# Where the second low part of Q stands in VectorE's list, before or after the two copies of the row maxima

## The chip, the cores and the metric

The kernel runs on one core of a Trainium2 chip. The metric is the device time of one execution in microseconds (us), as the median of several runs. The core's engines each work through a list of instructions of their own, in order, and meet only at semaphores: TensorE (PE in the profile), VectorE (DVE), ScalarE (ACT), GpSimd (POOL), and SyncE (SP), which here only issues DMAs.

## The reference

The input is 16 images of 64 x 64 positions with 256 channels. For each image the layer computes

```
h1 = n1_w * arcsinh(h) + n1_b
q, k, v = split(h1 @ qkv_w + qkv_b), q scaled by hd ** -0.5     # 8 heads of 32
attn = softmax over the 3 x 3 neighbours (clipped at the edge) of q . k
h  = h + (attn @ v) @ proj_w + proj_b
h2 = n2_w * arcsinh(h) + n2_b
out = h + gelu(h2 @ mlp_w1 + mlp_b1) @ mlp_w2 + mlp_b2          # exact gelu
```

Everything is float32. The kernel gets that precision out of float16 matmuls: each value is split into a high and a low float16 part, and a product is taken as high x high, high x low and low x high.

## The kernel before, in words

The images are cut into 128 bands of 8 rows (512 tokens). A band has 8 tiles of 8 x 8 queries, and each tile attends to a window of 10 x 10 keys; a mask inside the matmul takes out what is no neighbour. One step of the kernel (`step(t, u)`, one for each band) works on five bands at once: attention of band t, Q, K and V of band t+2, the first arcsinh of band t+3, projection, second arcsinh and first MLP product of band t-1, second MLP product and result of band t-2. A step has four slots (k = 0 to 3), each with two tiles. The order on each engine is written out by hand: every engine has its own `step`, and what it does in a slot stands there line by line. Nothing is reordered by a planner.

The change touches VectorE's `step` (lines 909 to 968), in the second slot (k = 1). There VectorE works through this list:

- `maximum`, `maximum_high`, `maximum_low` (lines 839 to 852): row maxima of the scores of the next two tiles, split into parts.
- `q_low(t + 2, par, 0)` (lines 805 to 811): the first low part of Q, that is Q in PSUM plus bias less its float16 high part, 128 partitions x 512.
- `sum_reciprocal` and `normalise` of tile 2 (lines 862 to 876). `normalise` is two operations: the first reads and writes partitions 0 to 63, the second partitions 64 to 127.
- `maxima_to_queries` (lines 854 to 860): two copies of the transposed maxima into the `queries` tile. Both write eight partitions from partition 96 on. The first reads PSUM from partition 0, the second from partition 32 (`MAX_STEP`). They wait for `pe_max`, the transpose of the maxima on TensorE.
- `q_low(t + 2, par, 1)`: the second low part of Q. It waits for `q_hi_ready`, the high part that ScalarE writes (line 1018).
- `x_from_transposes(t + 3, ..., 0)` and `(..., 1)` (lines 754 to 757): the two halves of the turned input, PSUM to SBUF.
- `sum2_` (line 763, called from 789), `v_low(t + 2, 0)`, tile 3's `sum_reciprocal` and `normalise`, `magnitude1` (line 760), `v_low(t + 2, 1)`.

The third slot begins with `maximum` and its two parts, and then `sign2` (line 767, called from 794), whose result GpSimd splits into `b_hi` and `b_lo` (lines 1157 to 1164) for the first MLP product.

TensorE's list for slot 1 (lines 649 to 697) is: scores, the two Q products, the weighted sum of tile 2, `max_rows` (line 559), `x_transposes(t + 3, 0)`, `v_product(t + 2, 0)`, `x_transposes(t + 3, 1)`, `v_product(t + 2, 1)`, the weighted sum of tile 3, and `scores_t`. The PSUM banks are shared: the second transposes write the bank that held the second half of Q, so they wait for `q_lo_ready` of `q_low(..., 1)` (line 400). The second V product writes the bank that held the first half of the turned input, so it waits for `xT_ready` of `x_from_transposes(..., 0)` (line 448).

ScalarE takes V's high parts (`v_high`, line 1049) behind the V products, then `probabilities` of tile 4 (lines 1058 to 1064: `prob` and `p_hi`), the logarithm `log2_`, and `probabilities` of tile 5. GpSimd forms `p_lo` of each tile behind `p_hi` (`p_low`, lines 1142 to 1146).

Of the kernel before, what the change touches and what calls it, by code (L numbers as in the profile page):

```python
# [108 lines left out]
def build(nc, x, qkv_w, qkv_b, proj_w, proj_b, n1_w, n1_b, n2_w, n2_b, mlp_w1, mlp_b1, mlp_w2, mlp_b2,  # L109
# [5 lines left out]
    with ExitStack() as ctx:  # L115
# [131 lines left out]
        def has(band):  # L247

            return not isinstance(band, int) or 0 <= band < BANDS

        def signals(t, per, n):


            return max(t * per + n, 0) if isinstance(t, int) else t * per + n
# [451 lines left out]
        def _(v):  # L706
# [47 lines left out]
            def x_from_transposes(t, u, g):  # L754

                v.wait_ge(pe_x, signals(t, G, g + 1))
                v.tensor_scalar(xT[u][:, g, :], ps[:, X_BANK[g], :], WS, None, ALU.mult).then_inc(xT_ready, 1)
# [22 lines left out]
            def sign1(t, u):  # L780
                v.wait_ge(log1, signals(t, 1, 1))
                with_sign(ln1_u[:], flat2(xT[u]), ln1_s[:], asinh1)
# [11 lines left out]
            def sign2(t, par):  # L794
                v.wait_ge(log2, signals(t, 1, 1))
                with_sign(ln2_u[:], flat2(h[par]), ln2_s[:], asinh2)

            def h_from_projection(t, par, u, g):

                v.wait_ge(pe_proj, signals(t, G, g + 1))  # L800
                v.wait_ge(pe_m2, signals(t - 2, 2, 2))
                v.scalar_tensor_tensor(out=h[par][:, g, :], in0=ps[:, PROJ_BANK[g], :], scalar=bp[:, g:g + 1],  # L802
                                       in1=xT[u][:, g, :], op0=ALU.add, op1=ALU.add).then_inc(h_ready, 1)

            def q_low(t, par, g):

                v.wait_ge(q_hi_ready, signals(t, G, g + 1))
                v.scalar_tensor_tensor(  # L808
                    out=q_nat[par][:, 1, g].rearrange("p c q -> p (c q)"), in0=ps[:, Q_BANK[g], :], scalar=bqk[:, g:g + 1],
                    in1=q_nat[par][:, 0, g].rearrange("p c q -> p (c q)"),  # L810
                    op0=ALU.add, op1=ALU.subtract).then_inc(q_lo_ready, 1)

            def k_low(t, g):
                v.wait_ge(k_hi_ready, signals(t, G, g + 1))
                v.scalar_tensor_tensor(  # L815
                    out=k_nat[:, 1, g, :, 1:1 + SIDE], in0=rows_of(ps[:, K_BANK[g], :]), scalar=bqk[:, G + g:G + g + 1],
                    in1=k_nat[:, 0, g, :, 1:1 + SIDE], op0=ALU.add, op1=ALU.subtract).then_inc(k_lo_ready, 1)
# [8 lines left out]
            def o_low(t, par, half):  # L826
                v.wait_ge(o_hi_ready, signals(t, 2, half + 1))
                v.tensor_tensor(turned(o_lo[par], half), turn_bank(half), turned(o_hi[par], half),
                                ALU.subtract).then_inc(o_lo_ready, 1)
# [9 lines left out]
            def maximum(t, k):  # L839
                v.wait_ge(pe_s, signals(t, SLOTS, k + 1))  # L840
                v.tensor_reduce(maxima_of_pair(),  # L841
                                ps[:, B_S:B_S + 2, 0:PAIRS * NK].rearrange("p n (a k) -> p n a k", k=NK),
                                AX.X, ALU.max).then_inc(max32_ready, 1)

            def maximum_high(t, k):
                v.wait_ge(max32_ready, signals(t, SLOTS, k + 1))
                v.tensor_scalar(max_columns(k, 0), maxima_of_pair(), MAX_SCALE, None, ALU.mult).then_inc(max_hi_ready, 1)

            def maximum_low(t, k):
                v.wait_ge(max_hi_ready, signals(t, SLOTS, k + 1))  # L850
                v.scalar_tensor_tensor(out=max_columns(k, 1), in0=maxima_of_pair(), scalar=MAX_SCALE, in1=max_columns(k, 0),
                                       op0=ALU.mult, op1=ALU.subtract).then_inc(max_ready, 1)

            def maxima_to_queries(t, par, k):
                v.wait_ge(pe_max, signals(t, SLOTS, k + 1))
                for n in range(2):
                    to = queries[par][MAX0:MASK0].bitcast(U32).rearrange("r g (m e) c q -> r (g m) e c q", e=2)[:, :, :, 2 * k + n, :]
                    rows = ps[MAX_STEP * n:MAX_STEP * n + MAX_ROWS, B_S, MAXT_COLS].bitcast(U32)
                    rows = rows.rearrange("r (a e q) -> r a e q", a=1, e=2)
                    v.tensor_copy(to, rows.to_broadcast([MAX_ROWS, PAIRS, 2, NQ // 2])).then_inc(maxima_placed, 1)  # L860

            def sum_reciprocal(t, c):
                v.wait_ge(pe_av, signals(t, TILES, c + 1))
                av = ps[:, B_AV, 0:VROW].rearrange("p (a w) -> p a w", w=VW)
                v.reciprocal(recip[c % 2][:], av[:, :, 2 * HD:VW]).then_inc(recip_ready, 1)

            def normalise(t, c):

                av = ps[:, B_AV, 0:VROW].rearrange("p (a w) -> p a w", w=VW)
                v.wait_ge(recip_ready, signals(t, TILES, c + 1))  # L870
                v.wait_ge(pe_ot, signals(t - 1, 2, c // (TILES // 2) + 1))
                for e in range(2):
                    r = slice(NQ * e, NQ * e + NQ)
                    s = v.tensor_tensor(o_norm[r, c], av[r, :, HD * e:HD * e + HD],  # L874
                                        recip[c % 2][r].to_broadcast([NQ, PAIRS, HD]), ALU.mult)
                s.then_inc(norm_ready, 1)
# [32 lines left out]
            def step(t, u):  # L909
                par, old = u % 2, 1 - u % 2  # L910
                att, pre, post, fin, fill = has(t), has(t + 2), has(t - 1), has(t - 2), has(t + 3)
                for k in range(SLOTS):
                    ta, ka = (t, k + 1) if k + 1 < SLOTS else (t + 1, 0)
                    more = has(ta)
                    if more:
                        maximum(ta, ka)
                        maximum_high(ta, ka)
                        maximum_low(ta, ka)

                    if k == 0 and post:  # L920
                        o_low(t - 1, old, 1)
                    if k == 0 and pre:
                        k_low(t + 2, 0)
                    if k == 1 and pre:
                        q_low(t + 2, par, 0)
                    if k == 2 and post:
                        sign2(t - 1, old)
                    if k == 3 and att:
                        o_low(t, par, 0)
                    if k == 3 and fill:  # L930
                        sign1(t + 3, (u + 3) % XT)

                    if att:
                        sum_reciprocal(t, 2 * k)
                        normalise(t, 2 * k)
                    if more:
                        maxima_to_queries(ta, par if ta == t else old, ka)

                    if k == 0 and pre:
                        k_low(t + 2, 1)  # L940
                    if k == 0 and post:
                        h_from_projection(t - 1, old, (u - 1) % XT, 0)
                        h_from_projection(t - 1, old, (u - 1) % XT, 1)
                    if k == 1 and pre:
                        q_low(t + 2, par, 1)
                    if k == 1 and fill:
                        x_from_transposes(t + 3, (u + 3) % XT, 0)
                        x_from_transposes(t + 3, (u + 3) % XT, 1)
                    if k == 1 and post:
                        sum2_(t - 1)  # L950
                    if k == 1 and pre:
                        v_low(t + 2, 0)
                    if k == 2 and fill:
                        sum1_(t + 3)
                    if k == 2 and fin:
                        result(t - 2, 0)

                    if att:
                        sum_reciprocal(t, 2 * k + 1)
                        normalise(t, 2 * k + 1)  # L960
                    if k == 0 and post:
                        magnitude2(t - 1, old)
                    if k == 1 and fill:
                        magnitude1(t + 3, (u + 3) % XT)
                    if k == 1 and pre:
                        v_low(t + 2, 1)
                    if k == 2 and fin:
                        result(t - 2, 1)
# [5 lines left out]
            for t in range(-3, 0):  # L974
                opening(t)
            run(step, 0)


# [261 lines left out]
```

## Time and profile before

| | |
|---|---|
| median of 3 runs | 4439.54 us (4438.06 to 4439.81) |
| the profiled execution, its own time | 4440.94 us |
| its span in the trace | 4439.1 us |
| TensorE busy | 4159.5 us, 94% |
| VectorE busy | 3926.1 us, 88% |
| ScalarE busy | 3631.7 us, 82% |
| GpSimd busy | 3359.0 us, 76% |
| a full step in the middle (`sign2` to `sign2`) | 33.73 us |

The profile is one execution; times in it are in us from the start of the span. A row of the timeline gives start, duration, engine, line, operation with the tiles that it writes and reads, and how many instructions it stands for; behind it, in brackets, how long the engine had been idle and who released it. The rows below are of the step between 2036.57 and 2070.31 us, which looks like nearly all the others, and of the end of the kernel, where work runs out. Spans of TensorE's matmuls overlap: the next one starts before the modelled end of the one before.

### The profile page before, as it was taken

The numbers are of one execution on the slowest core, as the hardware profiler recorded it, in microseconds if no ns is written. First come the engines' busy times: TensorE is split into PE (matmuls) and PEld (weight loads), VectorE is DVE, ScalarE is ACT, GpSimd is POOL, SyncE is SP. The second block draws the span as 40 slices with busy tenths as digits, with TensorE's granted clock in tenths as the row PEclk, the third lists the DMA queues.
The fourth block names the chain that finished last, engine by engine and source line by source line (L and its number), as shares of the span: only waits on it lengthen the run. The fifth ranks groups of instructions, "written<-read, shape, count | busy, mean of one in ns | idle before, by whom it ended". The sixth has DMA issues, their size and how long they took to land.

```text
span 4439.1 us, 129514 instructions
## 1 busy us (share of the span) xinstructions
PE 4159.5 (94%) x49224; PEld 2857.8 (64%) x49224; DVE 3926.1 (88%) x8225; ACT 3631.7 (82%) x5377; POOL 3359.0 (76%) x4092
## 2 busy tenths in 40 slices
PE   5999999999999999999999999999999999999997
PEld 3666666666666666666666666666666666666664
DVE  6899999989989998998999899899989989999984
ACT  4888888888888888888888888888888888888884
POOL 2777777777777777777777777777777777777775
PEclk8999999999999999999999999999999999999998
DMA  4555555555555555555555555555555555555551
GB/s 120 132 141 139 142 139 143 136 139 141 141 140 140 142 137 139 141 140 141 140 142 137 140 141 139 140 141 141 139 139 144 136 140 140 141 141 138 142 133 50
DMA packets 644105, 607.94 MB, mean 137 GB/s; under 512 B 77070, under 2 KB 639376, under 8 KB 639888
## 3 DMA queue, kind: packets, MB, share of 16 engines
q1 hardware_dynamic: 643488, 599.66, 51.2%
q8 instruction: 394, 6.46, 0.7%
q14 instruction: 223, 1.83, 0.1%
HBM read 206.02 MB, written 135.40 MB: 77 GB/s over the span
## 4 chain that ended last, share of the span: by engine, by line
DVE 42%; PE 18%; POOL 13%; issue 13%; ACT 12%; SPq 1%; DMA 0%; POOLq 0%; DVEq 0%; ACTq 0%
PE ps L381 16%; POOL b_lo L1163 6%; POOL b_hi L1161 6%; DVE ps L841 5%; DVE queries L860 5%; DVE o_norm L874 4%; DVE ln_u L767 4%; DVE ln_u L760 4%; DVE k_nat L815 4%; ACT L1073 4%; DVE ln_u L763 3%; DVE h L802 3%; ACT p_hi L1064 3%; DVE q_nat L808 3%; ACT prob L1063 2%
## 5 line engine op out<-in xcount | busy, mean ns | idle before, releaser
L1146 POOL TENSOR_TENSOR p_lo<-prob,p_hi 100x512 f16<-100x512 f32 x1024 | 1269.7, 1245 | 619.1 <-ACT p_hi L1064 619.1
L1063 ACT ACTIVATE prob<-ps 100x512 f32<-100x512 f32 x1024 | 610.2, 596 | 51.1 <-PE ps L381 49.3
L874 DVE TENSOR_TENSOR o_norm<-ps,recip 64x128 f32<-64x128 f32 x2048 | 590.2, 288 | 49.3
L1172 POOL TENSOR_TENSOR g_lo<-g,g_hi 128x512 f16<-128x512 f32 x512 | 593.8, 1160 | 41.0
L1064 ACT ACTIVATE p_hi<-ps 100x512 f16<-100x512 f32 x1024 | 616.4, 602 | 0.0
L381 PEld LDWEIGHTS ps<-v_win,p_hi 100*128 100x128 f16 x8192 | 476.0, 98 | 204.7 <-issue 66.9
L381 PE MATMUL ps<-w_hi,g_hi 128*128 128x256 f16 x2048 | 561.1, 274 | 0.0
L841 DVE TENSOR_REDUCE ps<-ps 128x8 f32<-128x800 f32 x512 | 509.1, 994 | 58.6 <-PE ps L381 54.2
L381 PE MATMUL ps<-w_lo,g_hi 128*128 128x256 f16 x2048 | 560.9, 274 | 0.0
L381 PE MATMUL ps<-w_hi,g_lo 128*128 128x256 f16 x2048 | 560.8, 274 | 0.0
L381 PE MATMUL ps<-v_win,p_hi 100*128 100x65 f16 x8192 | 515.6, 193 | 27.0 <-POOL p_lo L1146 18.4
L381 PE MATMUL ps<-v_win,p_lo 100*128 100x65 f16 x4096 | 481.8, 193 | 0.0
L860 DVE COPY queries<-ps 8x256 uint32<-8x256 uint32 x1024 | 429.2, 419 | 32.1 <-PE ps L559 0.4
L1040 ACT ACTIVATE k_win<-k_nat 128x640 f16<-128x640 f16 x512 | 349.4, 730 | 128.1 <-DVE k_nat L815 124.1
L381 PE MATMUL ps<-a_hi,wqkv_hi 128*128 128x512 f16 x1024 | 393.1, 384 | 59.0 <-POOL a_lo L1154 48.7
L381 PE MATMUL ps<-b_hi,w_hi 128*128 128x512 f16 x1024 | 393.7, 384 | 23.8 <-POOL b_lo L1163 23.7
L1161 POOL CAST b_hi<-ln_u 128x512 f16<-128x512 f32 x256 | 280.0, 1094 | 151.0 <-DVE ln_u L767 151.0
L381 PE MATMUL ps<-a_lo,wqkv_hi 128*128 128x512 f16 x1024 | 390.2, 381 | 0.0
L381 PE MATMUL ps<-a_hi,wqkv_lo 128*128 128x512 f16 x1024 | 389.9, 381 | 0.0
L381 PE MATMUL ps<-b_lo,w_hi 128*128 128x512 f16 x1024 | 389.8, 381 | 0.0
L381 PE MATMUL ps<-b_hi,w_lo 128*128 128x512 f16 x1024 | 389.6, 380 | 0.0
L381 PEld LDWEIGHTS ps<-v_win,p_lo 100*128 100x128 f16 x4096 | 382.2, 96 | 0.0
(100 smaller groups left out, 11497.9 us busy)
## 6 DMA issues: line engine op xcount, KB each, us to landing
keys<-k_win SPq DMA_DIRECT2D x1536, 100.0 KB, 2.3
v_win<-v_rows SPq DMA_DIRECT2D x1024, 101.6 KB
queries<-q_nat SPq DMA_DIRECT2D x1536, 64.0 KB
v_rows<-v_nat SPq DMA_DIRECT2D x256, 260.0 KB, 4.3
xin<-in_x_dram SPq DMA_DIRECT2D x128, 512.0 KB, 4.3
out_dram<-y SPq DMA_DIRECT2D x256, 256.0 KB, 3.0
queries<-in_query_mask_dram SPq DMA_DIRECT2D x128, 224.0 KB
keys<-in_mlp_w_dram SPq DMA_DIRECT2D x2, 512.0 KB, 6.5
```

Of the source, the lines that this page charges most:

```text
L381: return pe.matmul(o, a, b, start=start, stop=stop, skip_group_check=True)
L760: v.tensor_single_scalar(out.bitcast(U32), of.bitcast(U32), MAGNITUDE, ALU.bitwise_and).then_inc(s, 1)
L841: v.tensor_reduce(maxima_of_pair(), ps[:, B_S:B_S + 2, 0:PAIRS * NK].rearrange("p n (a k) -> p n a k", k=NK), AX.X, ALU.max).then_inc(max3 ...
L860: v.tensor_copy(to, rows.to_broadcast([MAX_ROWS, PAIRS, 2, NQ // 2])).then_inc(maxima_placed, 1)
L874: s = v.tensor_tensor(o_norm[r, c], av[r, :, HD * e:HD * e + HD], recip[c % 2][r].to_broadcast([NQ, PAIRS, HD]), ALU.mult)
L1040: s = act.activation(to[:, :, 1:1 + TS], rows, ACT.Copy)
L1063: act.activation(prob[b][0:NK], ps[0:NK, B_ST + b, :], ACT.Exp, scale=INV * INV).then_inc(prob_ready, 1)
L1064: act.activation(p_hi[b][0:NK], ps[0:NK, B_ST + b, :], ACT.Exp, scale=INV * INV).then_inc(p_hi_ready, 1)
L1146: pool.tensor_tensor(p_lo[b][0:NK], prob[b][0:NK], p_hi[b][0:NK], ALU.subtract).then_inc(p_lo_ready, 1)
L1161: pool.tensor_copy(b_hi[:, g, :], ln2_u[:, g * TOK:(g + 1) * TOK]).then_inc(b_hi_ready, 1)
L1163: pool.tensor_tensor(b_lo[:, g, :], ln2_u[:, g * TOK:(g + 1) * TOK], b_hi[:, g, :], ALU.subtract).then_inc(b_lo_ready, 1)
L1172: pool.tensor_tensor(g_lo[:, m, :], g32[:, m, :], g_hi[:, m, :], ALU.subtract).then_inc(g_lo_ready, 1)
```

## The change

In slot 1 of VectorE's step the call of `q_low(t + 2, par, 1)` moves up, from behind `maxima_to_queries` to in front of it. Nothing else is touched; the same instructions are issued.

```diff
@@ -933,6 +933,8 @@
                     if att:
                         sum_reciprocal(t, 2 * k)
                         normalise(t, 2 * k)
+                    if k == 1 and pre:
+                        q_low(t + 2, par, 1)
                     if more:
                         maxima_to_queries(ta, par if ta == t else old, ka)
 
@@ -941,8 +943,6 @@
                     if k == 0 and post:
                         h_from_projection(t - 1, old, (u - 1) % XT, 0)
                         h_from_projection(t - 1, old, (u - 1) % XT, 1)
-                    if k == 1 and pre:
-                        q_low(t + 2, par, 1)
                     if k == 1 and fill:
                         x_from_transposes(t + 3, (u + 3) % XT, 0)
                         x_from_transposes(t + 3, (u + 3) % XT, 1)
```

## Rows read from the trace of the kernel before

**Rows 1.** Waits of TensorE: total us, times, longest us

```profile
PE ps L405 <- DVE q_nat L808: 113.7, 125, 0.9
```

**Rows 2.** Waits of VectorE, same columns

```profile
DVE xT L757 <- PE ps L405: 22.8, 129, 1.9
```

**Rows 3.** Timeline of VectorE from the second slot's normalisation on

```profile
2048.25 0.59 DVE L874 TENSOR_TENSOR o_norm<-ps,recip 64x128 f32<-64x128 f32 x2
2048.87 0.87 DVE L860 COPY queries<-ps 8x256 uint32<-8x256 uint32 x2
2049.78 0.75 DVE L808 SCALAR_TENSOR_TENSOR q_nat<-ps,bqk,q_nat 128x512 f16<-128x512 f32 x1
2050.44 0.68 DVE L757 TENSOR_SCALAR xT<-ps 128x512 f32<-128x512 f32 x1
2051.27 0.69 DVE L757 TENSOR_SCALAR xT<-ps 128x512 f32<-128x512 f32 x1 [0.15 <-PE ps L405]
2051.88 1.22 DVE L763 SCALAR_TENSOR_TENSOR ln_u<-ln_u,ln_s 128x1024 f32<-128x1024 f32 x1
2053.01 0.69 DVE L822 SCALAR_TENSOR_TENSOR v_nat<-ps,v_nat 128x512 f16<-128x512 f32 x1
```

**Rows 4.** Timeline of TensorE: transposes, V products, then the next scores

```profile
2047.63 0.63 PE L405 MATMUL ps<-ident,xin 128*128 128x128 f32 x4
2048.19 0.28 PE L381 MATMUL ps<-wqkv_hi,a_hi 128*128 128x256 f16 x1
...
2049.40 0.27 PE L381 MATMUL ps<-wqkv_hi,a_lo 128*128 128x256 f16 x1
2050.58 0.66 PE L405 MATMUL ps<-ident,xin 128*128 128x128 f32 x4 [0.91 <-DVE q_nat L808]
2051.18 0.28 PE L381 MATMUL ps<-wqkv_hi,a_hi 128*128 128x256 f16 x1
...
2052.87 0.63 PE L381 MATMUL ps<-queries,keys 124*128 124x64 f16 x16
```

**Rows 5.** Timeline of ScalarE: second high part of Q, of V, `p_hi` of tile 5

```profile
2048.02 0.71 ACT L1018 ACTIVATE q_nat<-ps,bqk 128x512 f16<-128x512 f32 x1
...
2052.70 0.60 ACT L1049 ACTIVATE v_nat<-ps 128x512 f16<-128x512 f32 x1 [1.45 <-PE ps L381]
...
2055.70 0.61 ACT L1064 ACTIVATE p_hi<-ps 100x512 f16<-100x512 f32 x1
```

**Rows 6.** Timeline of GpSimd: `p_lo` of tile 5, `b_hi`, `p_lo` of tile 7

```profile
2056.39 1.17 POOL L1146 TENSOR_TENSOR p_lo<-prob,p_hi 100x512 f16<-100x512 f32 x1 [0.24 <-ACT p_hi L1064]
2058.70 0.61 POOL L1161 CAST b_hi<-ln_u 128x512 f16<-128x512 f32 x1 [1.14 <-DVE ln_u L767]
...
2065.24 1.16 POOL L1146 TENSOR_TENSOR p_lo<-prob,p_hi 100x512 f16<-100x512 f32 x1 [0.31 <-ACT p_hi L1064]
```

**Rows 7.** Timeline of VectorE: `sign2`, `sum1_` and what follows it, `sign1`

```profile
2057.08 1.55 DVE L767 SCALAR_TENSOR_TENSOR ln_u<-h,ln_s 128x1024 uint32<-128x1024 uint32 x1
...
2060.29 1.34 DVE L763 SCALAR_TENSOR_TENSOR ln_u<-ln_u,ln_s 128x1024 f32<-128x1024 f32 x1
2061.66 0.69 DVE L835 SCALAR_TENSOR_TENSOR y<-ps,b 128x512 f32<-128x512 f32 x1
...
2065.61 1.86 DVE L767 SCALAR_TENSOR_TENSOR ln_u<-xT,ln_s 128x1024 uint32<-128x1024 uint32 x1
```

**Rows 8.** Timeline of VectorE near the end of the kernel: another `sign2`

```profile
4316.22 1.21 DVE L767 SCALAR_TENSOR_TENSOR ln_u<-h,ln_s 128x1024 uint32<-128x1024 uint32 x1
```

**Rows 9.** Timeline of GpSimd at the same place: `p_lo` of tile 5

```profile
4315.10 1.16 POOL L1146 TENSOR_TENSOR p_lo<-prob,p_hi 100x512 f16<-100x512 f32 x1 [1.02 <-ACT p_hi L1064]
```

**Rows 10.** Chain that ended last, by time: start, us, what (three of its pieces)

```profile
2040.14 0.56 DVE k_nat L815
...
2063.39 2.49 PE ps L381 x21
...
2068.72 0.02 ACT g L1071
```

## The prediction, made before the changed kernel was run

> **What bounds the kernel now.** I read the waits first, then one step's timeline engine by engine, then the chain. TensorE is the busiest engine, but it is not full: its largest wait, 113.7 us in 125 waits of 0.9, is for VectorE's second low part of Q [rows 1]. The reader is to see what the change aims at: normalisation, two copies, low part stand one behind the other, and only the low part releases the second transposes, at 2050.58 [rows 3, 4]. So the low part could come 0.91 us earlier (2048.87 in place of 2049.78), and TensorE's idle 0.91 seems to be for the taking.
>
> The next line of TensorE's list says no. The second V product starts at 2051.18. It needs the first half of xT out of its bank, and that operation ends at 2050.44 + 0.68 = 2051.12 [rows 3]; 0.06 later the product starts. The same 0.05 lies between the end of the low part (2049.78 + 0.75 = 2050.53) and the transposes at 2050.58. Both are releases by VectorE. A second sign: the first transposes let their successor start after 0.56 (2047.63 to 2048.19), the second ones after 0.60 [rows 4]; the 0.04 is the wait for xT. Nobody sees it in the list of waits, because the transposes stood in front of it.
>
> From there I follow the loop to find out what a change of that moment is worth:
> - V product 2051.18, ScalarE's second high part of V at 2052.70, which had waited 1.45 for it; then ScalarE runs without a gap through tile 4 and the logarithm to p_hi of tile 5, 2055.70 + 0.61 = 2056.31 [rows 5].
> - GpSimd's p_lo of tile 5 waits for that (idle 0.24), runs 2056.39 to 2057.56 [rows 6].
> - VectorE's sign2 is recorded from 2057.08 with 1.55 us [rows 7]. The same operation took 1.21 where p_lo had only 0.04 left (4315.10 + 1.16 = 4316.26, sign2 at 4316.22) [rows 8, 9]. It ends 1.07 behind p_lo's end (2058.63 less 2057.56). sign1 on the same line began when its p_lo had 0.79 left, took 1.86, and ended 1.07 behind it (2067.47 less 2066.40) [rows 6, 7]. So these operations with two SBUF inputs stand still until GpSimd has finished, and then need about 1.1: the end of sign2 is set by p_lo of tile 5, not by when VectorE arrives.
> - sign2's end releases b_hi at 2058.70 (idle 1.14) [rows 6]; b_lo releases TensorE at 2063.39, that releases the last gelu at 2068.72, and over the activation table, the probabilities and K's high part it comes back to VectorE's k_low (2040.14 in this step), from which VectorE runs without a gap to the normalisation of rows 3 [rows 10].
>
> That closes the loop: first half of xT, V product, ScalarE, p_lo, sign2, GpSimd, TensorE, ScalarE, k_low, normalisation, copies and low part, first half of xT. VectorE's own way, from the second half of xT to sign2, is beside it: it arrives at 2057.08 and could be served only about 0.4 later (1.55 against 1.21 is 0.34 of standing still).
>
> The Trainium skill ("SBUF — State Buffer", SBUF: two separate sides) has this as a rule: the port pair that VectorE and GpSimd share is an exclusive lock held for a whole instruction, also against a VectorE operation with two SBUF inputs. By that rule, and the rows agree, VectorE's earlier arrival is worth nothing; with a shared bandwidth instead, part of it would be kept.
>
> **The change part by part.** It adds and removes no instruction; SP's and GpSimd's lists are untouched.
>
> (a) The low part moves up by 0.91. It needs ScalarE's high part, which ends at 2048.02 + 0.71 = 2048.73 [rows 5]; VectorE is free at 2048.84, so 0.1 is to spare, and ScalarE's place relative to VectorE is fixed by k_low. The second transposes can start at 2048.87 + 0.75 + 0.05 = 2049.67; TensorE's product before them has its last start at 2049.40 [rows 4]. So TensorE's wait for Q all but goes: 0.91 x 125 = 114 us of idle time. What is late next is the V product's wait for the first half of xT, behind transposes that end near 2050.3. The idle time moves there whole: worth 0.
>
> (b) The copies come later by 0.78. Who needs them is TensorE's scores_t at 2052.87, behind the weighted sum [rows 4]; the copies end near 2050.5. More than 2 us are to spare: 0. Without that cover the cost would be the 0.78.
>
> (c) The sum from the normalisation's end to the start of the first half of xT. It would be unchanged if operations followed one another at the same distance in either order, and they do not. Behind copies and normalisations the next operation starts 0.03 after the end (2048.84 to 2048.87, 2049.74 to 2049.78). Behind the low part, the first xT copy with nothing to wait for starts 0.09 before the recorded end (2050.53 to 2050.44), and V's low part so behind sum2_ (2053.10 to 2053.01) [rows 3]. The trace before shows no copy of maxima behind a low part, so its gap is bounded by these: -0.09 to +0.03.
> Which? It could hang on the operation in front (low part: overlap) or on a change of the partitions where operands start. Against the first: sum1_ is the same operation as sum2_, yet V's low part overlaps sum2_, while the result's operation (L835) starts 0.03 after sum1_ ends (2061.63 to 2061.66) [rows 7]; what differs is that before L835 PSUM was last read by a copy from partition 32. And the first half of a normalisation starts at partition 0, as the low part does, while its second half starts at 64: the pair takes 0.59 with two operations of 0.29, no overlap [rows 3]. The copies write from partition 96. I take +0.03.
> Then: now 0.87 for the copies, 0.75 for the low part, gaps 0.03 + 0.03 - 0.09: 2050.44. After: low part 2048.87 to 2049.62, copies 2049.65 to 2050.52, first half of xT at 2050.52 + 0.03 = 2050.55. The one overlap in the stretch is lost: +0.11 (0 at the other bound).
>
> The Trainium skill ("VectorE: DVE Perf Modes", Two Vector instructions with no wait between them) describes held instructions: one whose output or input starts in another group of 32 partitions than the last one in that memory starts only when all before it have finished. By it the copy behind the low part is held and the stretch is longer by the same 0.11; read by the operation in front alone, it would be 0. No row of before has that pair itself.
>
> (d) VectorE's own branch: the second half of xT no longer waits 0.15 for the transposes (22.8 us in all [rows 2]); it starts 0.61 behind the first (the distance from it to sum2_ in rows 3), at 2051.16 in place of 2051.27. 0.11 earlier; with the other bound of (c), 0.22. It ends at sign2, which then stands still longer: worth 0.
>
> Sum: +0.11 on the loop, in each of the 125 steps that have this wait: 0.11 x 125 = 13.8 us. Against the profiled execution, 4440.94 + 13.8 = 4454.7; the median of the runs is 1.4 lower, 4439.54 + 13.8 = 4453.3. All links of the loop are releases with 0.02 to 0.08 between end and start, so I expect nearly all of the 0.11 to show; rounding of each gap (0.01) makes it 0.08 to 0.13, or 10 to 16 us.
>
> **The rivals.**
> No change (0.20): the copy overlaps the low part, as every operation behind a low part does in the trace before; the first half of xT stays at 2050.44 and the loop with it: 4439.5. For it: the -0.09 behind the low part. Against it: the two pairs in (c). A milder form with the same result is that a link of the loop has some 0.1 to spare that I did not see.
> Faster (0.08): VectorE's own branch decides. The chain of waits as printed speaks for it: it runs from the low part through the transposes and the second half of xT to sign2. Then 0.11 to 0.22 a step comes through, 14 to 27 us: 4412 to 4426. It decides if sign2's end follows its start; the three pairs in rows 6 to 9, with one distance to p_lo's end for two arrivals, speak against it. The whole 0.91, 4439.5 - 114 = 4326, would need the V product not to wait for xT: I give it less than 0.01 of this.
> Not doing what it says: if the high part of Q came late, the low part would stand in front of the copies and hold them and xT. It has 0.1 to spare; 0.1 late would add 0.1 a step (12 us on top). I put it at 0.02, within the slower side.
>
> **How the numbers follow.** 4453.3 is the likeliest case, 0.70 with its own range 4449 to 4457. About 0.2% (8.9 us) is what a measurement of this kernel can tell from no change. Slower by more than that: 0.72 with the late high part. Within: 0.20. Faster: 0.08. The range from 4438 to 4458 takes in both bounds of (c) and leaves out the faster rival and the late high part, a little over 0.1.
>
> **What would show each step right or wrong.** In the changed profile: TensorE's wait for the low part of Q is gone from its list, and a wait for xT (L757) of about 0.9 to 1.0, 125 times, stands in its place. The second transposes follow V's first product directly. The copies start 0.03 behind the low part's end (0.09 before it would show the rival), and the first half of xT starts 1.71 behind the end of the normalisation, now 1.60. VectorE's wait for the transposes (22.8 us) is gone. sign2 is recorded longer, about 1.77 for 1.55, and still ends 1.07 behind p_lo. The step is 33.84 in place of 33.73. I am wrong if the step is as long as before or shorter; a sign2 of 1.55 that simply starts earlier would say that the branch beside the loop was the bound.

## The result: 0.36% slower, and the profile after

The changed kernel takes 4455.1 us (median of 6, 4454.29 to 4455.88) against 4438.8 us (median of 6, 4436.32 to 4441.92) for the kernel before; the ratio is 1.0036, 95% interval 1.0023 to 1.0049. The forecast was 4453.3 us, slower. The span of the profiled execution went from 4439.1 to 4452.5 us, 13.4 more, where the working had 13.8.

The waits of TensorE in the changed kernel come first (total us, times, longest us), the list in which the change shows most plainly. The wait for the low part of Q [rows 1] is gone from the head of it, and a wait for the first half of xT has its place:

```profile
PE ps L381 <- DVE xT L757: 121.0, 125, 1.0
PE ps L381 <- POOL a_lo L1154: 48.2, 124, 1.3
```

Then the timeline of VectorE over the same stretch as [rows 3] (start, duration, engine, line, operation):

```profile
2054.93 0.59 DVE L874 TENSOR_TENSOR o_norm<-ps,recip 64x128 f32<-64x128 f32 x2
2055.56 0.75 DVE L808 SCALAR_TENSOR_TENSOR q_nat<-ps,bqk,q_nat 128x512 f16<-128x512 f32 x1
2056.34 0.87 DVE L860 COPY queries<-ps 8x256 uint32<-8x256 uint32 x2
2057.24 1.29 DVE L757 TENSOR_SCALAR xT<-ps 128x512 f32<-128x512 f32 x2
2058.44 1.21 DVE L763 SCALAR_TENSOR_TENSOR ln_u<-ln_u,ln_s 128x1024 f32<-128x1024 f32 x1
...
2063.65 1.79 DVE L767 SCALAR_TENSOR_TENSOR ln_u<-h,ln_s 128x1024 uint32<-128x1024 uint32 x1
```

The low part starts at once behind the normalisation. The copies start 0.03 behind its end (2056.31 to 2056.34), not 0.09 ahead of it. The first half of xT starts at 2057.24, 1.72 behind the normalisation's end (2055.52); before it was 1.60 [rows 3]. The two halves of xT now follow each other with no wait between them.

TensorE, to be held against [rows 4]: the second transposes start early, and the product behind them stands still.

```profile
2056.07 0.27 PE L381 MATMUL ps<-wqkv_hi,a_lo 128*128 128x256 f16 x1
2056.36 0.66 PE L405 MATMUL ps<-ident,xin 128*128 128x128 f32 x4
2057.99 0.28 PE L381 MATMUL ps<-wqkv_hi,a_hi 128*128 128x256 f16 x1 [0.97 <-DVE xT L757]
```

GpSimd, to be held against [rows 6], with p_lo of tiles 4 and 5:

```profile
2061.27 1.45 POOL L1146 TENSOR_TENSOR p_lo<-prob,p_hi 100x512 f16<-100x512 f32 x1 [2.85 <-ACT p_hi L1064]
2063.19 1.16 POOL L1146 TENSOR_TENSOR p_lo<-prob,p_hi 100x512 f16<-100x512 f32 x1 [0.47 <-ACT p_hi L1064]
2065.50 0.61 POOL L1161 CAST b_hi<-ln_u 128x512 f16<-128x512 f32 x1 [1.15 <-DVE ln_u L767]
```

The reader is to see sign2 (the L767 above): VectorE came to it earlier within the step, and it is recorded with 1.79 in place of 1.55. It ends at 2065.44, 1.09 behind p_lo's end at 2064.35; before, the distance was 1.07 [rows 6, 7]. What VectorE saved on its own branch is spent standing still. From `sign2` to `sign2` the step is 33.85, before 33.73.

### The profile page after: what moved, and what is told of

It is laid out like the page before. It is cut to its first block, busy times and chain, and to the rows that moved or that the text cites. A ratio compares the mean times of both kernels' runs of the same rounds, so it can differ in the third digit from the quotient of the medians.

```text
span 4452.5 us, 129514 instructions
## 1 busy us (share of the span) xinstructions
PE 4163.9 (94%) x49224; PEld 2854.1 (64%) x49224; DVE 3956.8 (89%) x8225; ACT 3628.7 (81%) x5377; POOL 3326.5 (75%) x4092
## 4 chain that ended last, share of the span: by engine, by line
DVE 46%; PE 16%; POOL 13%; issue 12%; ACT 12%; SPq 1%; DMA 1%; POOLq 0%; DVEq 0%; ACTq 0%
PE ps L381 16%; POOL b_lo L1163 6%; POOL b_hi L1161 6%; DVE ps L841 5%; DVE ln_u L767 5%; DVE queries L860 5%; DVE o_norm L874 4%; DVE ln_u L760 4%; DVE k_nat L815 4%; ACT L1073 4%; DVE h L802 3%; DVE ln_u L763 3%; ACT p_hi L1064 3%; DVE q_nat L808 3%; DVE v_nat L822 3%
## 5 line engine op out<-in xcount | busy, mean ns | idle before, releaser
L1146 POOL TENSOR_TENSOR p_lo<-prob,p_hi 100x512 f16<-100x512 f32 x1024 | 1239.6, 1215 | 663.8 <-ACT p_hi L1064 663.8
L381 PE MATMUL ps<-wqkv_hi,a_hi 128*128 128x256 f16 x1024 | 282.0, 275 | 122.3 <-DVE xT L757 121.0
```

The lines of the kernel that those rows point to most:

```text
L381: return pe.matmul(o, a, b, start=start, stop=stop, skip_group_check=True)
L1146: pool.tensor_tensor(p_lo[b][0:NK], prob[b][0:NK], p_hi[b][0:NK], ALU.subtract).then_inc(p_lo_ready, 1)
```

## The experiments

All kernels are edits of the kernel before; one adds to another edit, and the text says so. Times are given with the ratio to the kernel before, run on the same chip. Median of the kernel before: 4441.53 us in the first group of four, 4438.62 us in the second.

**Is the first half of xT what counts?** The low part and the first half of xT both go in front of the copies.

```diff
+                    if k == 1 and pre:
+                        q_low(t + 2, par, 1)
+                    if k == 1 and fill:
+                        x_from_transposes(t + 3, (u + 3) % XT, 0)
                     if more:
                         maxima_to_queries(ta, par if ta == t else old, ka)
...
-                    if k == 1 and pre:
-                        q_low(t + 2, par, 1)
                     if k == 1 and fill:
-                        x_from_transposes(t + 3, (u + 3) % XT, 0)
                         x_from_transposes(t + 3, (u + 3) % XT, 1)
```

> The second low part of Q and the first half of xT both in front of the copies of the maxima. My theory (a loop through the first half of xT, the second V product, ScalarE, p_lo and sign2, with VectorE's own branch some 0.34 us beside it): the first half of xT starts near 2049.53 in the frame of the step shown, 0.91 earlier than before, the V product at 2050.27 instead of 2051.18, and the 0.9 us idle of TensorE is gone. Then the loop no longer binds and VectorE's branch does: sign2 no longer stands still behind p_lo. If magnitude1 (L760) is not stopped by p_lo of tile 4, the step shortens by 0.45 to 0.5 (56 to 62 us, about 4380); if it is stopped, as p_lo comes before it now, it loses about 0.3 and the step shortens by 0.15 to 0.25 (19 to 31 us, 4408 to 4420). Rival, that the branch through the transposes was the bound before: at most 0.13 a step, 4423. Rival, that the swap itself costs and the place of xT doesn't matter: 4453 as in the changed kernel.

Measured: 4415.79 us, ratio 0.9943 (0.9930 to 0.9956), 25.7 us faster than before. VectorE and then GpSimd in that kernel:

```profile
2038.50 0.59 DVE L874 TENSOR_TENSOR o_norm<-ps,recip 64x128 f32<-64x128 f32 x2
2039.13 0.75 DVE L808 SCALAR_TENSOR_TENSOR q_nat<-ps,bqk,q_nat 128x512 f16<-128x512 f32 x1
2039.80 0.68 DVE L757 TENSOR_SCALAR xT<-ps 128x512 f32<-128x512 f32 x1
2040.51 0.87 DVE L860 COPY queries<-ps 8x256 uint32<-8x256 uint32 x2
...
2044.58 0.95 DVE L760 TENSOR_SCALAR ln_u<-xT 128x1024 uint32<-128x1024 uint32 x1
2045.56 0.69 DVE L822 SCALAR_TENSOR_TENSOR v_nat<-ps,v_nat 128x512 f16<-128x512 f32 x1
2046.17 0.99 DVE L841 TENSOR_REDUCE ps<-ps 128x8 f32<-128x800 f32 x1
...
2047.48 1.22 DVE L767 SCALAR_TENSOR_TENSOR ln_u<-h,ln_s 128x1024 uint32<-128x1024 uint32 x1
```

```profile
2043.82 1.16 POOL L1147 TENSOR_TENSOR p_lo<-prob,p_hi 100x512 f16<-100x512 f32 x1 [1.82 <-ACT p_hi L1065]
2045.74 1.16 POOL L1147 TENSOR_TENSOR p_lo<-prob,p_hi 100x512 f16<-100x512 f32 x1 [0.76 <-ACT p_hi L1065]
```

The first half of xT starts 0.71 behind the normalisation's end in place of 1.60, sign2 takes 1.22, so it waits for nobody, and magnitude1 (L760) takes 0.95 for 0.69 because p_lo of tile 4 (2043.82 to 2044.98) is under way. That is the second of the two outcomes that I had given for my theory, in the middle of its 4408 to 4420; both rivals (4423 at best, and 4453) are out.

TensorE's idle time has moved once more. The wait for xT is gone, and a third one heads the list, for V's first low part (L822), at the start of the second MLP product (L535):

```profile
PE ps L535 <- DVE v_nat L822: 81.8, 124, 1.4
```

**What does a change of start partition cost?** One spare operation at one place on the loop, in two kernels that differ in its first partition alone (here 96; the other has 0).

```diff
+        spare = sb("spare", [P, 64], U32)
...
                     if k == 1 and fill:
+                        v.memset(spare[96:96+8], 0)
                         x_from_transposes(t + 3, (u + 3) % XT, 0)
                         x_from_transposes(t + 3, (u + 3) % XT, 1)
```

> The kernel before with one spare memset of 8 partitions x 64 words between the second low part of Q and the first half of xT, starting at partition 0; it is on the loop. Nothing of the result changes. A memset of 128 x 64 took 0.11 us; with the overlap of 0.09 on both sides its net price is 0.02 to 0.03 a step, 2 to 4 us: 4441 to 4443. Every theory says this; it is the base for the next one.

> The same spare memset at the same place, starting at partition 96. If a change of the partitions where operands start makes an operation wait for the end of the one before, both neighbouring overlaps are lost: 0.03 + 0.11 + 0.03 + 0.09 = 0.26 a step, 32 us: about 4471, some 29 us above the run with partition 0. If the gap depends on the kind of the operation in front alone, it takes the same time as with partition 0, 4441 to 4443. If what stands before the first half of xT is not on the loop, both stay at 4439.

Measured: from partition 0 4442.66 us, 1.0002 (0.9992 to 1.0011); from partition 96 4476.27 us, 1.0077 (1.0064 to 1.0090). The difference is 33.6 us, 0.27 in each of 125 steps. First the kernel with partition 0, then the one with 96:

```profile
2052.62 0.75 DVE L809 SCALAR_TENSOR_TENSOR q_nat<-ps,bqk,q_nat 128x512 f16<-128x512 f32 x1
2053.32 0.11 DVE L948 MEMSET spare<- 8x64 uint32 x1
2053.36 0.62 DVE L758 TENSOR_SCALAR xT<-ps 128x512 f32<-128x512 f32 x1
```

```profile
2068.77 0.75 DVE L809 SCALAR_TENSOR_TENSOR q_nat<-ps,bqk,q_nat 128x512 f16<-128x512 f32 x1
2069.59 0.11 DVE L948 MEMSET spare<- 8x64 uint32 x1
2069.72 0.69 DVE L758 TENSOR_SCALAR xT<-ps 128x512 f32<-128x512 f32 x1
```

Same operation, same size, same neighbours. The distances are taken from the recorded ends. From partition 0 it starts 0.05 before the low part's end, and xT 0.07 before its own end; xT ends 1.36 behind the low part's start (before, 1.34). From partition 96 it starts 0.07 behind the low part's end and xT 0.02 behind its own: 1.64. As the kind of the operation is the same in both, the start partition makes the difference. It costs 0.12 on the way in (the memset starts 0.82 behind the low part's start, not 0.70) and 0.16 on the way out (xT ends 0.82 behind the memset's start, not 0.66), 0.28 in all. In the kernel with partition 96 TensorE now has a wait that the other doesn't list:

```profile
PE ps L382 <- DVE xT L758: 29.1, 125, 0.2
```

These two runs do not tell a change of the start partition from a high partition that is slow in itself; the next run has a row on that.

**The same operation beside the loop.** At the end of the second slot, behind V's second low part and in front of the next slot's reduction (L842 here), still ahead of sign2.

```diff
                     if k == 1 and pre:
                         v_low(t + 2, 1)
+                    if k == 1 and fill:
+                        v.memset(spare[96:96+8], 0)
```

> The same spare memset from partition 96, behind the second low part of V at the end of the second slot: between the first half of xT and sign2, on VectorE's own branch beside the loop. My theory: the 0.26 us (0.17 to 0.26, since the operation behind it is a reduction that reads from partition 0) is swallowed by the time in which sign2 stands still; sign2 is recorded some 0.2 to 0.26 shorter (about 1.3 for 1.55), still ends 1.07 behind p_lo, and the time is that of before, within 3 us. Rival, that VectorE's branch is the bound: 0.2 to 0.26 a step, 25 to 32 us slower, 4464 to 4471.

Measured: 4441.37 us, 1.0000 (0.9991 to 1.0009). The same memset that costs 34.7 us on the loop costs nothing here. VectorE, then GpSimd:

```profile
2056.85 0.11 DVE L969 MEMSET spare<- 8x64 uint32 x1
2056.89 0.93 DVE L842 TENSOR_REDUCE ps<-ps 128x8 f32<-128x800 f32 x1
...
2058.14 1.42 DVE L768 SCALAR_TENSOR_TENSOR ln_u<-h,ln_s 128x1024 uint32<-128x1024 uint32 x1
```

```profile
2057.31 1.17 POOL L1149 TENSOR_TENSOR p_lo<-prob,p_hi 100x512 f16<-100x512 f32 x1 [0.23 <-ACT p_hi L1067]
```

sign2 is 0.13 shorter than before (1.42 for 1.55) and ends 1.08 behind p_lo (2059.56 less 2058.48). I had expected 0.2 to 0.26 of delay to be swallowed; only 0.13 arose. The reason can be seen in the reduction: it reads and writes PSUM alone, and starts 0.07 before the memset's end, although the memset started at partition 96. So partition 96 does not by itself stop what comes behind it. The first half of xT, which writes to SBUF from partition 0, did wait for the same memset. That fits a change of the start partition within one memory. For the way in no run decides: none has a memset from partition 96 behind an operation that starts at 96 too.

**One place earlier on the same branch.** The same memset between the second half of xT and `sum2_`.

```diff
                         x_from_transposes(t + 3, (u + 3) % XT, 1)
+                        v.memset(spare[96:96+8], 0)
```

> The kernel before with the spare memset from partition 96 between the second half of xT and sum2_, on VectorE's branch beside the loop, but ahead of magnitude1 (L760). Before, magnitude1 starts 0.03 us before p_lo of tile 4 and p_lo waits for it. With 0.25 more in front of it p_lo comes first. My theory (a single-source operation from SBUF to SBUF is stopped too until GpSimd's is over, then needs 0.55 more): magnitude1 ends near 2056.18, 1.05 later than before, sign2 arrives at 2058.1 with p_lo of tile 5 already done, takes 1.21 and ends 0.7 later: about 85 us slower, 4525, from a memset of 0.11 us which at the end of the slot cost nothing. Rival, that the order in which the two arrive doesn't matter (shared bandwidth): the 0.25 is swallowed as at the other place, 4441.

Measured: 4527.39 us, 1.0199 (1.0183 to 1.0214), 88.8 us slower. First magnitude1 and p_lo of tile 4 in the kernel before, then VectorE and GpSimd in this one:

```profile
2054.44 0.69 DVE L760 TENSOR_SCALAR ln_u<-xT 128x1024 uint32<-128x1024 uint32 x1
2054.47 1.68 POOL L1146 TENSOR_TENSOR p_lo<-prob,p_hi 100x512 f16<-100x512 f32 x1 [2.69 <-ACT p_hi L1064]
```

```profile
2057.92 0.69 DVE L758 TENSOR_SCALAR xT<-ps 128x512 f32<-128x512 f32 x1 [0.15 <-PE ps L406]
2058.68 0.11 DVE L950 MEMSET spare<- 8x64 uint32 x1
...
2061.38 1.44 DVE L761 TENSOR_SCALAR ln_u<-xT 128x1024 uint32<-128x1024 uint32 x1
...
2064.77 1.21 DVE L768 SCALAR_TENSOR_TENSOR ln_u<-h,ln_s 128x1024 uint32<-128x1024 uint32 x1
```

```profile
2061.11 1.16 POOL L1148 TENSOR_TENSOR p_lo<-prob,p_hi 100x512 f16<-100x512 f32 x1 [2.71 <-ACT p_hi L1066]
```

In the kernel before, magnitude1 starts 0.03 ahead of p_lo and runs its 0.69, and p_lo is the one that takes longer (1.68 for 1.16). Its lead is 0.02 or 0.03 in each of the 124 steps where the two meet. Here p_lo of tile 4 began 0.27 before magnitude1, so magnitude1 stands still for 0.75 (1.44 for 0.69) and ends 0.55 behind it. The memset and its gaps add 0.29 (magnitude1 starts 3.46 behind the start of the second half of xT, before 3.17), which makes 1.04 of delay; 0.34 of it is swallowed at sign2 (now 1.21), and 0.70 a step is left (88.8 / 125 = 0.71). The rival, that the order of arrival doesn't matter, gave 4441 and is out.

**The first half of xT moved up alone.**

```diff
+                    if k == 1 and fill:
+                        x_from_transposes(t + 3, (u + 3) % XT, 0)
                     if more:
                         maxima_to_queries(ta, par if ta == t else old, ka)
...
                     if k == 1 and fill:
-                        x_from_transposes(t + 3, (u + 3) % XT, 0)
                         x_from_transposes(t + 3, (u + 3) % XT, 1)
```

> The kernel before with only the first half of xT moved in front of the copies; the second low part of Q stays behind them. My theory: VectorE's order is normalisation, first half of xT, copies, low part. In the frame of before the low part then ends near 2051.2 in place of 2050.5, the second transposes start near 2051.26 and the V product at 2051.82, behind the transposes, 0.64 to 0.66 later than before. TensorE's wait for the low part comes back as 1.6 a step, and the loop gets longer by 0.64 to 0.66: 80 to 83 us, about 4522. Rival, that moving xT up is good in itself: near the 4416 of the run with both moved. Rival, that VectorE's branch is the bound: the transposes release the second half of xT at 2051.9, 0.65 later, and the stand-still of 0.34 would not be used up: also slower, but by 0.65 only if nothing is swallowed.

Measured: 4601.55 us, 1.0366 (1.0352 to 1.0380), 162.9 us slower: twice my 80 to 83. TensorE's first wait, VectorE, then GpSimd:

```profile
PE ps L405 <- DVE q_nat L808: 203.8, 125, 1.6
```

```profile
2123.00 0.69 DVE L757 TENSOR_SCALAR xT<-ps 128x512 f32<-128x512 f32 x1
2123.72 0.87 DVE L860 COPY queries<-ps 8x256 uint32<-8x256 uint32 x2
2124.62 0.75 DVE L808 SCALAR_TENSOR_TENSOR q_nat<-ps,bqk,q_nat 128x512 f16<-128x512 f32 x1
2126.12 0.69 DVE L757 TENSOR_SCALAR xT<-ps 128x512 f32<-128x512 f32 x1 [0.75 <-PE ps L405]
...
2129.29 1.62 DVE L760 TENSOR_SCALAR ln_u<-xT 128x1024 uint32<-128x1024 uint32 x1
```

```profile
2129.20 1.16 POOL L1147 TENSOR_TENSOR p_lo<-prob,p_hi 100x512 f16<-100x512 f32 x1 [3.30 <-ACT p_hi L1065]
```

The direction and the wait of 1.6 for the low part came as expected. What I had left out was the race that the run before this one in the text shows: relative to the normalisation's end the second half of xT, and magnitude1 with it, comes 0.72 later, but p_lo of tile 4 only 0.60 later (6.23 behind it for 5.63). So the lead of 0.03 turns into 0.09 behind, and magnitude1 is stopped (1.62 for 0.69). 0.72 + 0.93 - 0.34 = 1.31 a step, 164 us. I had priced the loop and not the branch that came to overtake it. The run also shows that xT early is not enough: the low part has to be early as well.

**V's second low part in front of magnitude1**, once on the kernel before, once on the kernel with low part and first half of xT up.

```diff
-                    if k == 1 and fill:
-                        magnitude1(t + 3, (u + 3) % XT)
                     if k == 1 and pre:
                         v_low(t + 2, 1)
+                    if k == 1 and fill:
+                        magnitude1(t + 3, (u + 3) % XT)
```

> The kernel before with only V's second low part in front of magnitude1. magnitude1 now starts behind p_lo of tile 4's start, is stopped until p_lo is over and ends near 2056.18. VectorE's branch comes to sign2 some 0.33 later, just the time that sign2 had stood still: sign2 is recorded with about 1.22 and ends where it did. My theory: no change, 0 to 3 us slower. Rival, that VectorE's branch is the bound: 0.33 a step, 41 us slower, 4480. Rival, that the swap of these two is good in itself: 0.38 a step faster, 4392.

> The kernel with low part and first half of xT in front of the copies (4415.8), and V's second low part in front of magnitude1. In that kernel magnitude1 is recorded with 0.95 in place of 0.69, stopped by p_lo of tile 4, and VectorE's branch is the bound. My theory: magnitude1 now comes when p_lo is over (saves 0.27), and it and the reduction behind it no longer change the partitions they read from (one held start less, 0.11): 0.38 a step, 47 us, about 4368; a part may be lost if p_lo of tile 5 is now in the way or the next loop binds: 4366 to 4395. Rival, that the loop found for before still binds: no change, 4416.

Measured: on the kernel before 4438.51 us, 0.9999 (0.9990 to 1.0008): no change. On the kernel with both moves 4365.48 us, 0.9835 (0.9822 to 0.9848), 73.1 us faster than before. The kernel with both moves alone gained 25.7, so 47.4 us come from this last edit (each gain taken against the kernel before in its own group; the intervals leave some 8 us either way), and 47 were expected. That kernel beats both kernels of the comparison. VectorE and GpSimd's p_lo of tile 5 with the edit alone, then VectorE in the kernel with all three moves:

```profile
2055.82 1.12 DVE L760 TENSOR_SCALAR ln_u<-xT 128x1024 uint32<-128x1024 uint32 x1
...
2058.17 1.22 DVE L767 SCALAR_TENSOR_TENSOR ln_u<-h,ln_s 128x1024 uint32<-128x1024 uint32 x1
```

```profile
2057.16 1.15 POOL L1146 TENSOR_TENSOR p_lo<-prob,p_hi 100x512 f16<-100x512 f32 x1 [0.76 <-ACT p_hi L1064]
```

```profile
2053.01 0.69 DVE L822 SCALAR_TENSOR_TENSOR v_nat<-ps,v_nat 128x512 f16<-128x512 f32 x1
2053.62 0.68 DVE L760 TENSOR_SCALAR ln_u<-xT 128x1024 uint32<-128x1024 uint32 x1
2054.22 0.99 DVE L841 TENSOR_REDUCE ps<-ps 128x8 f32<-128x800 f32 x1
...
2055.53 1.22 DVE L767 SCALAR_TENSOR_TENSOR ln_u<-h,ln_s 128x1024 uint32<-128x1024 uint32 x1
```

Alone, magnitude1 is stopped and VectorE comes to sign2 0.33 later, but sign2 stands still 0.33 less (1.22 for 1.55) and ends 1.08 behind p_lo (2059.39 less 2058.31): the time that the branch had to spare, used up and not exceeded. With the loop out of the way the same edit is worth 1.1%, 0.38 a step. Of that, 0.27 is magnitude1's stop (0.68 for 0.95). The other 0.11 is one overlap won between the low part of V and magnitude1: in the kernel with both moves the second of the two starts 0.03 after the first one's end (2045.53 to 2045.56), now 0.08 before it (2053.70 to 2053.62). The reduction behind the pair overlaps by 0.08 in either order; my expectation had counted it among the operations that change.

## Why the prediction was right

- **(a) The wait for Q goes and comes back as a wait for xT.** Right: 113.7 us in 125 waits [rows 1] became 121.0 us in 125. The second transposes start 0.84 behind the normalisation's end (before, 1.74); the V product starts 0.07 behind the end of xT's first half (2057.24 + 0.68), before 0.06.
- **(b) The copies have time.** Right: no wait of TensorE for them came up among its large ones (2.0 us in 4 waits in the whole run).
- **(c) The lost overlap, +0.11.** Right: +0.12, with a gap of +0.03 or +0.04 behind the low part in every step. Before the run this was a choice between two bounds; the changed kernel and the two memsets have now shown it. The rule cited for it there (the Trainium skill, "VectorE: DVE Perf Modes", Two Vector instructions with no wait between them) is borne out by the two memsets, 33.6 us apart by the start partition alone. The loop passes it on in full: 0.12 x 125 = 15 us, measured 13.4 by the spans and 16.3 by the medians (10 to 22 by the interval).
- **(d) VectorE's own branch, worth nothing.** Right: its wait for the transposes [rows 2] went from 22.8 to 4.4 us, sign2 got longer by 0.24 (expected 0.22) and ends at the same distance to p_lo. Delays of 0.13 and 0.33 on the branch cost nothing, one of 1.04 costs all but 0.34. The spare time read from the trace, 0.34, fits the three runs.
- **The faster rival** had the chain of waits as printed on its side. That chain runs through sign2 with its whole recorded duration, and doesn't show that part of it is standing still. It was wrong for this reason.

Not tried: taking the collision of sign2 with p_lo away while all else stays. Nor did a run move one of the loop's links behind sign2 (GpSimd, TensorE, the last gelu, k_low): they are read from the trace alone. What the runs show is that a delay in front of xT's first half comes through whole (0.28 in the rows, 0.27 a step).

## What to carry to other kernels

A wait at the head of the list hides the ones behind it: before pricing it, look at what the next instructions on that engine wait for, and when those are released. An operation that takes longer than its twin elsewhere (1.55 and 1.86 for 1.21) may be standing still for another engine, so that what comes ahead of it is beside the critical loop, and what sets the other engine's end is on the loop. Where small operations on a few high partitions stand between wide ones, count the borders at which the start partition changes in the memory that the next operation uses: moving one such block can add a border, and each cost 0.11 to 0.16 us here.

## What the runs showed of the hardware that was not expected

A lead of 0.03 us of one engine over another can carry tens of us: magnitude1 led p_lo by that much, and the kernel lost 88.8 us when 0.29 was put in front of magnitude1. Delays between 0.03 and 0.29 were not tried there. One memset of 0.11 us costs 0, 34.7 or 88.8 us (0, 0.8 or 2.0%) at three places of the same slot. The prediction had looked at sign2 alone; VectorE's 32-bit operation from SBUF to SBUF with one source (L760, 0.69 for the same 1024 columns) is stopped by GpSimd's p_lo just as the one with two sources is: it ended 0.55 behind p_lo's end in the three kernels above where both rows stand (2045.53 less 2044.98 with both moved up, 2062.82 less 2062.27 with the early memset, 2130.91 less 2130.36 with xT alone), and when it comes first p_lo waits (1.68 for 1.16 in the kernel before, 1.45 in the changed one).
